# The third activation layer of a sandwich block: rounded copies made by a VectorE cast in place of a second Gelu on ScalarE

## What is computed

```python
x = x + layernorm(attention(layernorm(x), W_qkv))
u = layernorm(x)
h = silu(u @ w1.T * w1_s) * (u @ w2.T * w2_s)     # 128 -> 512, called A1 below
h = gelu(h @ h1.T * h1_s)                         # 512 -> 512, called A2
h = gelu(h @ h2.T * h2_s)                         # 512 -> 512, called A3
y = h @ w3.T * w3_s                               # 512 -> 128
x = x + layernorm(y)
```

## Time and profile before

| | us |
|---|---|
| median of 3 runs | 134.03 (133.97 to 134.73) |
| the profiled execution, its own device time | 134.5 |
| its span, first to last instruction of the program | 132.6 |
| busy PE / PEld / DVE / ACT / POOL | 125.5 / 103.3 / 104.7 / 98.5 / 28.3 |

### The profile page before, as it was taken

One profiled execution on the slowest core, in us unless ns is written; L12 is line 12 of the kernel. 1 busy time (PEld: TensorE's weight loads), 2 busy tenths in 40 slices (PEclk: granted clock), 3 DMA queues, 4 the chain that ended last, 5 costly groups with the idle time before them and its releaser, 6 DMA issues. The chain is left out here.

```text
span 132.6 us, 2374 instructions
## 1 busy us (share of the span) xinstructions
PE 125.5 (95%) x699; PEld 103.3 (78%) x699; DVE 104.7 (79%) x356; ACT 98.5 (74%) x184; POOL 28.3 (21%) x39
## 2 busy tenths in 40 slices
PE   6999998999989999999999999999999999999970
PEld 4685968889876888887889888888776788789960
DVE  1769599999899998938799999566989973996433
ACT  3128779878799919389999277799991996996640
POOL 4281330034210013400200174300002530000352
PEclk9999999999999999999999999999999999999996
DMA  4899997000200000000000001020000002000002
GB/s 112 262 278 405 374 374 240 0 0 5 82 0 5 0 5 2 0 0 0 5 0 0 0 5 40 2 79 7 0 0 0 0 0 84 0 5 0 2 29 94
DMA packets 5344, 8.28 MB, mean 62 GB/s; under 512 B 464, under 2 KB 2768, under 8 KB 5328
## 3 DMA queue, kind: packets, MB, share of 16 engines
q1 hardware_dynamic: 3984, 5.19, 12.3%
q0 software_dynamic: 1344, 2.88, 6.6%
HBM read 7.02 MB, written 1.05 MB: 61 GB/s over the span
## 5 line engine op out<-in xcount | busy, mean ns | idle before, releaser
L317 POOL TENSOR_TENSOR rstd<-ve,minus_half 128x4 f32<-128x4 f32 (+1 forms) x19 | 18.5, 974 | 92.7 <-DVE ve L678 51.6
L1147 PE MATMUL F<-a_hi,h_hi 128*128 128x512 f32 (+1 forms) x160 | 37.7, 357 | 0.0
L1153 PE MATMUL F<-a_lo,h_hi 128*128 128x512 f32 (+1 forms) x160 | 37.3, 353 | 0.1
L610 DVE TENSOR_TENSOR a_lo<-act_full,a_hi 128x512 fp32r<-128x512 f32 (+1 forms) x52 | 30.0, 604 | 3.7 <-ACT act_full L427 3.2
L435 ACT ACTIVATE a_hi<-F,sc 128x512 fp32r<-128x512 f32 (+1 forms) x35 | 21.1, 625 | 14.6 <-PE F L1153 14.5
L1153 PEld LDWEIGHTS F<-a_lo,h_hi 128*128 128x128 f32 x160 | 26.8, 188 | 5.4 <-DVE a_lo L610 1.1
L1147 PEld LDWEIGHTS F<-a_hi,h_hi 128*128 128x128 f32 x160 | 26.0, 188 | 4.5 <-DVE a_hi L716 0.6
L427 ACT ACTIVATE act_full<-F,sc 128x512 f32<-128x512 f32 (+1 forms) x40 | 23.3, 619 | 1.0 <-PE F L1153 1.0
L708 DVE SCALAR_TENSOR_TENSOR act_full<-F,sc,silu 128x512 f32<-128x512 f32 (+1 forms) x16 | 10.7, 681 | 1.7 <-ACT silu L416 1.4
L1104 PE MATMUL F<-x2T_hi,w_hi 128*128 128x512 f32 (+1 forms) x32 | 10.3, 404 | 0.5 <-DVE x2T_lo L610 0.3
L416 ACT ACTIVATE silu<-F,sc 128x512 f32<-128x512 f32 (+1 forms) x16 | 9.8, 634 | 0.9 <-PE F L1107 0.7
(11 more groups left out here) (154 smaller groups left out, 197.5 us busy)
## 6 DMA issues: line engine op xcount, KB each, us to landing
h_raw<-h SPq DMA_DIRECT2D x2, 1024.0 KB, 11.4
h_hi<-h POOLq DMA_DIRECT2D x2, 1024.0 KB, 8.7
xs<-x SPq DMA_DIRECT2D x3, 256.0 KB, 3.7
out<-outs SPq DMA_DIRECT2D x3, 256.0 KB, 2.2
w_raw<-w SPq DMA_DIRECT2D x1, 512.0 KB, 6.6
w_hi<-w POOLq DMA_DIRECT2D x1, 512.0 KB, 7.4
xs<-x SPq DMA_DIRECT2D x2, 128.0 KB, 7.8
w_raw<-w SPq DMA_DIRECT2D x1, 256.0 KB, 15.1
```

What stands on the lines that cost most here:

```text
L317: nc.gpsimd.tensor_tensor(rstd[:, ln, tiles(b)], ve[:, ln, tiles(b)], minus_half[:, 0:SIZES[b]], ALU.pow).then_inc(rstd_ready[ln], 1)
L610: nc.vector.tensor_tensor(dst, full, hi.bitcast(f32), ALU.subtract).then_inc(done, 1)
L1147: nc.tensor.matmul(out, terms[k][0], terms[k][2], start=(k == 0), stop=False)
L1153: last = [nc.tensor.matmul(out, terms[k][0], terms[k][3], start=False, stop=(k == KT - 1)) for out, terms in groups]
```

## The change

For all 16 slices of A3 in blocks 0 to 3, ACT runs one Gelu (the full value), and DVE makes the rounded copy with `high` directly ahead of `low`. One slice was so already, so 15 `gelu_high` leave ACT's list and 15 casts enter DVE's: 4 of 128x256 and 11 of 128x512. The rounded slices are counted by `third_cast` alone. `high` waits for its input buffer at every slice and not at slice 0 only. PE's list, the transfers and everything else stay. (A2 keeps its two Gelus.)

```diff
-        CAST_SLICES = 1
+        CAST_SLICES = (0, 1, 2, 3, 4, 5, 6, 7, 8, 9, 10, 11, 12, 13, 14, 15)
 
         def hi_done(n, b, o):
-            if n < A3 or b < LAST - 1:
-                return a_hi_ready[n], KT * b + o + 1
-            if o < CAST_SLICES:
-                return third_cast, o + 1
-            return a_hi_ready[A3], KT * b + o + 1 - CAST_SLICES
+            i = KT * b + o
+            if n < A3:
+                return a_hi_ready[n], i + 1
+            if i in CAST_SLICES:
+                return third_cast, CAST_SLICES.index(i) + 1
+            return a_hi_ready[A3], i + 1 - sum(k < i for k in CAST_SLICES)
...
-            gelu_high(A3, 0, 0)
             gelu(A3, 0, 0)
-            gelu_high(A3, 0, 1)
             gelu(A3, 0, 1)
             x2T_high(1)
-            gelu_high(A3, 0, 2)
-            gelu_high(A3, 0, 3)
             gelu(A3, 0, 2)
             gelu(A3, 0, 3)
...
-            gelu_high(A3, 1, 0)
             y_normalised(0)
-            gelu_high(A3, 1, 1)
             x2T_high(2)
             gelu(A3, 1, 0)
-            gelu_high(A3, 1, 2)
...
             def high(n, b, o):
                 c = slice(0, width(b))
-                if b > 0 and o == 0:
+                if b > 0:
                     dve.wait_ge(*a_used(n, b))
...
             x2T_low(1)
+            high(A3, 0, 0)
             low(A3, 0, 0)
             x_normalised(3)
             pT_copy(2, 0)
             maxima(2, 1)
+            high(A3, 0, 1)
             low(A3, 0, 1)
             gate(1, 0)
             gate(1, 1)
             high(A1, 1, 0)
             high(A1, 1, 1)
+            high(A3, 0, 2)
             low(A3, 0, 2)
             low(A1, 1, 0)
+            high(A3, 0, 3)
             low(A3, 0, 3)
             pT_copy(2, 1)
             low(A1, 1, 1)
...
             x2T_low(2)
+            high(A3, 1, 0)
             low(A3, 1, 0)
+            high(A3, 1, 1)
             low(A3, 1, 1)
+            high(A3, 1, 2)
             low(A3, 1, 2)
             x_statistics(4)
             v_copy(3)
             gT_copy(3)
+            high(A3, 1, 3)
             low(A3, 1, 3)
...
+            high(A3, 3, 1)
             low(A3, 3, 1)
+            high(A3, 3, 2)
             low(A3, 3, 2)
+            high(A3, 3, 3)
             low(A3, 3, 3)
             w3_scale()
             low(A2, 4, 0)
```

More of the change, by code:

```diff
@@ L519, in _ @@
             gelu(A2, 1, 3)
-            gelu_high(A3, 1, 0)
             y_normalised(0)
-            gelu_high(A3, 1, 1)
             x2T_high(2)
             gelu(A3, 1, 0)
-            gelu_high(A3, 1, 2)
             gelu(A3, 1, 1)
             gelu(A3, 1, 2)
-            gelu_high(A3, 1, 3)
             gelu(A3, 1, 3)
@@ L546, in _ @@
             y_normalised(1)
-            gelu_high(A3, 2, 0)
-            gelu_high(A3, 2, 1)
             gelu(A3, 2, 0)
@@ L551, in _ @@
             x2T_high(3)
-            gelu_high(A3, 2, 2)
             gelu(A3, 2, 2)
-            gelu_high(A3, 2, 3)
             gelu(A3, 2, 3)
@@ L576, in _ @@
             gelu(A3, 3, 0)
-            gelu_high(A3, 3, 1)
             gelu(A3, 3, 1)
-            gelu_high(A3, 3, 2)
-            gelu_high(A3, 3, 3)
             gelu(A3, 3, 2)
@@ L899, in _ @@
             x1_normalised(3)
+            high(A3, 2, 0)
             low(A3, 2, 0)
+            high(A3, 2, 1)
             low(A3, 2, 1)
             x2T_low(3)
+            high(A3, 2, 2)
             low(A3, 2, 2)
@@ L905, in _ @@
             v_copy(4)
+            high(A3, 2, 3)
             low(A3, 2, 3)
```

## The result

| | before | after |
|---|---|---|
| median of the runs, us | 134.03 (133.97 to 134.73) | 136.84 (136.51 to 137.25) |
| ratio to before, 95% interval | | 1.021 (1.017 to 1.025) |
| profiled execution / its span, us | 134.5 / 132.6 | 137.25 / 135.4 |

What follows compares the result with a forecast made beforehand. PE, busy 95% of the span, was taken as the bound, delayed only where it waits on DVE results. 1.14 + 0.33 - 0.45 + 1.03 = 2.05 us on the 134.03 median gave 136.1 us, range 134.7 to 137.0.

Steps and rivals of the forecast that it cites:

- Place 1: Blocks 0 to 1: casts delay PE at up(1,2) by 0.78 us, then 0.36 more at begin(A1,1); term +1.14.
- Place 2: Blocks 1 to 2: x2T_low(2) starts 0.62 us earlier, three pairs come in, scores(3,0) is held; term +0.33 us.
- Place 3: Blocks 2 to 3: ACT's relief reaches PE at attend(4,0) and A1's low slices; term -0.45 us.
- the second rival: ACT's relief wins: gains of 0.45 us at place 3 and about 0.2 at begin(A1,4); 133.4 us, chance 0.07.
- Place 4: Blocks 3 to 4: three pairs delay the last low that PE reads in end(A3,3); term +1.03 us.
- a pair dearer by 0.1 us: Upper bound: 0.63 and 0.50 us per pair if the extra buffer wait shows; 3.0 us in sum, 137.0.
- The pair: On DVE, a cast directly ahead of its low takes 0.53 us of queue for 128x512, 0.40 for 128x256.
- The pair at its own distance: Rival: wait inside the pair is free, 0.33 and 0.20 us each; sum 0.7, time 134.7, chance 0.12.
- The relief wins: Rival: DVE's queue takes up the casts at places 1 and 4, only gains are left; 133.4 us, chance 0.07.
- The delay runs on: Rival: DVE's lateness feeds on itself in blocks 2 and 3; if half comes through 3.7 us, 137.7, chance 0.13.

Runs made afterwards that it cites:

- relief alone: Against the kernel before: 15 second Gelus removed, no casts added, rounded tile filled once; by GpSimd copy 137.66 us (1.022), by transfer 133.66 us (0.998).
- act_shifted: Changed kernel with six more long-fulfilled waits in ACT's list alone, right ahead of gelu(A3,0,0); 136.71 us, ratio 1.020.
- no_block0: Changed kernel with slices 0 to 3 (block 0) keeping both Gelus on ACT and no cast; 135.53 us, ratio 1.009.
- the staggered order: Changed kernel with block 3's casts and lows reordered so that no low stands directly behind its own cast; 136.65 us, ratio 1.019.
- the kernel with both lists moved: Changed kernel with 18 more long-fulfilled waits in DVE's list and 6 more in ACT's; 136.93 us, ratio 1.021.

## Why the forecast was right, and where its size was off

**Place 1, 1.14 forecast, 1.41 measured.** The mechanism and both steps stand: two pairs ahead of G(1,0), released by the gate, then 0.33 more (0.36 forecast) ahead of begin(A1,1). The term that was mis-sized is the start of x2T_low(1). It was credited with 0.02 for the Gelus that went from ahead of x2T_high(1), and it became 0.3 us later. PE waits for it directly (0.61 us before, 0.91 after, at probs_transposes). That wait was in the trace of before and not in the forecast, which took up(1,2) for the first instruction of PE that is held here. The kernels with the relief alone have this +0.29 too, and without the pause (act_shifted) the place costs 1.13 us.

**Place 2, 0.33 forecast, 0.40 measured.** The relief (0.63), the distance to the copy (5.54) and the slack stand within 0.1 us.

**Place 3, -0.45 forecast, -0.31 measured**, the same in every kernel in which block 2's Gelus go (-0.30 to -0.33). G(3,2) and the lows do get earlier, but PE gains less than the sum of its small stretches: with block 2 alone 0.09 us at attend(4,0), where 0.11 was taken, and 0.13 us at A1's low slices, where 0.3 was; some 0.06 came at probs_transposes(4,0), which was not named. The other gain, 0.2 us at begin(A1,4), was named with the second rival and left out of the sum. It is real (-0.28), and leaving it out did no harm, because place 4 gives it back.

**Place 4, 1.03 forecast; 1.69 measured, or 1.41 net of the 0.28 that PE came earlier.** A PE that comes earlier to the same DVE result waits the longer, so the gain at begin(A1,4) is given back here. Measured from gate(4,2), the end of the last `low` moved from 6.65 to 8.59 us: 1.94 = 3 x 0.53 + 0.35. The three pairs are as forecast; the 0.35 is the pause ahead of slice 12's `low`. Without it (no_block0) the move is 8.24 - 6.65 = 1.59 = 3 x 0.53, and the place costs 1.34, net of the early arrival 1.04.

In sum, 2.92 - 2.05 = 0.87: 0.27 at place 1 and 0.35 at place 4 are the pauses, 0.14 is place 3, 0.07 place 2, and the -0.28 at begin(A1,4) and its return at place 4 cancel. The pauses were no term of the forecast. That 136.84 lies in the range is in part luck: its upper end, 137.0, was worked out for a pair dearer by 0.1 us, the pair was as forecast, and the time came near that end by the pauses. The trace of before has transfers of the "instruction" queue too, so their kind could have been seen in it, but not what one costs an engine, nor where they would fall in lists of another length.

**The pair.** 0.53 us (0.52 to 0.53 in the rows) and 0.40 us (0.38 to 0.40) held everywhere but where the pause stands inside it. The rule of the Trainium skill (page "VectorE: DVE Perf Modes", section "The DRAIN you can't avoid"), by which the semaphore inside a chained pair costs nothing extra, would have given 0.7 us in sum; three staggered pairs came out 0.59 us cheaper than three direct ones, and the rule doesn't hold for this case.

**The rivals.** *The pair at its own distance* is refuted by the staggered order. *The relief wins*: refuted, the relief alone is worth 0.3 us. *The delay runs on*: refuted, undoing block 0 leaves the terms of places 2 and 3 as they were and changes place 4 only by the pause. The traced sum, 2.9 us, lies between the forecast's 2.05 and that rival's 3.7, but for another reason, and only the kernels with one block undone tell the two apart.

**Side forecasts.** DVE busy near 110: 110.8. ACT near 89: 91.5. Busy time is a union, and a Gelu overlaps its neighbours, so what a removed one takes away is nearer to its distance of 0.57 us than to its 0.70 us.

## What to carry to other kernels

Moving work from an engine that waits to one that is idle a fifth of its time is priced by neither's busy time: here 6 us more on one and 7 us less on the other came to 2.9 us. Taking the few instructions of PE that start right behind a DVE result, and counting what is put ahead of them, gave the mechanism at all four places and 2.05 us, 0.1 to 0.4 us off at each place. A gain ahead of a tight place shrinks the slack in which a later cost was to lie, so gains and costs are to be followed in order of time and not added. Where a reader and its writer are neighbours on one engine, put something between them before deciding that the operation is too dear; and take the work only where the cover is (block 2 here).

## What the runs showed of the hardware

- Neighbours on DVE start 0.53 us apart where the second reads what a cast of 128x512 writes, and 0.33 us apart where it doesn't. An instruction whose own wait is the last starts 0.03 to 0.04 us after its release; one behind a separate wait instruction some 0.10 us.
- ACT and DVE pause at some positions of their instruction lists: 0.30 us at x2T_high(1), 0.36 us at slice 12's `low`, 0.14 us at 47.57 in the kernel with both lists moved. Not every 8 KB transfer of kind "instruction" comes with a pause (none at 116.47 with block 0 undone). A few instructions more or less anywhere ahead move the pause, and it can fall on a critical stretch in a later block (1.69 against 1.34 us at place 4, by an edit in block 0).
- A GpSimd copy of 128x2048, 1.90 us long, held a DVE instruction of 0.34 us for 2.58 us at the start, and with PE's lower clock after it the kernel stood 3.6 us behind at 35.1.
